# Two attention blocks on one core: regrouping DMAs split over two queues, the local projection moved ahead, and results of the next-to-last image moved

## The chip, the cores and the metric

One Trainium2 chip; the kernel runs on one of its cores. The metric is device time in microseconds, the median over runs of the same program.

## The reference, cut to what matters

The input x is 8 images of 32 x 32 tokens with 256 channels, float32. Two blocks follow each other, each behind a group norm (32 groups of 8 channels over all tokens of an image) and each added to its input.

```
x = x + local(gn(x))     # 32 rows of 32 tokens, 8 heads of 32: softmax(q k^T / sqrt(32)) v per row and head, then w_proj, b_proj
x = x + gamma * wide(gn(x))   # over all N = 1024 tokens of an image:
#   q = x Wq, k = x Wk (256 -> 32), v = x Wv (256 -> 256)
#   energy[i, j] = k_i . q_j;  attn = softmax over j;  out_i = sum_j attn[i, j] v_j
```

## The kernel before, in words

The kernel is written engine by engine, with semaphores placed by hand; each engine runs its own list in order, so the order of work is the order of the code. Products are made of float16 halves: a value is held as a high part and a low part, and a product takes three matmuls (`split3`, L275 to L277). PSUM is used as two tensors of four banks, pa and pb.

The local block is called a, the wide one b. For an image, block a has: load (SP), transposes and group norm ("a"), keys and queries (`a_project_qk`, chunks 0 and 1 of 512 tokens, four column groups d each; d = 0, 1 are queries and are copied by ScalarE, d = 2, 3 are keys and are copied by VectorE), values (`a_project_v`), scores, softmax, results (`a_output`), then the **regrouping**: VectorE ends the low parts of the results (`a_out_low`, L1010), and sixteen DMAs of 64 KB (`a_regroup`, L335, four r by four s) move them from the buffer before_turn to the buffer turned, so that channels lie on partitions. Then comes the **local projection** (`a_projection`, four groups j of 12 matmuls, form pa<-wp_h,turned), and the residual (`a_residual`, L1019, VectorE), which makes x1.

Block b takes x1: transposes and group norm ("b": statistics and aggregation L941 and L947, mean and variance over groups as two small matmuls on TensorE, L436 and L441, the scale on GpSimd, the normalisation on ScalarE, the split on VectorE L974 and L976), keys and queries (`b_project_qk`), the stacks (`b_stacks`, four DMAs), eight energy pairs (`b_energy`, L589), of which VectorE takes the row maxima (`b_maximum`, L1039; pair it + 1 waits for the maximum of pair it, since they share the banks), the maxima as two rows, eight transposed energy pairs (`b_energy_T`, L607), of which ScalarE takes the exponential (L833, L834) and VectorE the low part e_l (`b_exp_low`, L1054), values (`b_project_v`), and eight results (`b_output`, for each tile `it` of 128 rows 8 x 3 matmuls of 257 columns over `jt`), scaled by ScalarE (`b_scaled`, L843, with VectorE's factor, L1059 and L1061) and added by GpSimd (`b_add`, L1251) to y, into which GpSimd has copied x1 (`b_keep`, L1244). The stores of y are issued in pairs j of tiles by SP (j = 0, 1, 2) and ScalarE (j = 3); `b_keep` of pair j waits for the store of the image before.

Images overlap. `all_steps` calls two half-steps for i, `first(i)` and `second(i)`, on every engine. `first(i)` has energies of image i beside results of image i - 1, local results of image i + 1 and the norm of image i + 2; `second(i)` has transposed energies and values of image i, regrouping, local projection, norm b of image i + 1, and keys, queries, values and scores of image i + 2. i = 0, 1 are written out, i = 2, 3, 4 are a hardware loop (`Fori`, L246), i = 5 to 8 are written out again. The flags b, o, m, f of the half-steps say whether the images i, i - 1, i + 1, i + 2 exist. The last image is treated apart: its results 0 to 5 are made jt by jt right behind the exponentials (`outputs_behind`), in banks that are free by then (`result_bank`).

Lines that the steps below touch: `result_bank` L282, `a_regroup` L326, SP's half-steps L367 to L380, `a_projection` L546, `b_output` L611, TensorE's half-steps L632 to L701, ScalarE's L845 to L884, VectorE's L1063 to L1118, GpSimd's L1253 to L1271.

Of the kernel before, what the change touches and what calls it, by code (L numbers as in the profile page):

```python
# [55 lines left out]
def build(nc, x, w_qkv, w_proj, b_proj, wq1, wk1, wv1, gamma, ident_d, group_d, masks_d, out):  # L56
# [3 lines left out]
    with ExitStack() as ctx:  # L60
# [123 lines left out]
        a_ox = sem("a_ox")  # L184

# [95 lines left out]

        def result_bank(b, it):  # L282
# [58 lines left out]
        def _(sp):  # L341
# [53 lines left out]
            a_regroup(sp, 0, (0, 1))  # L395
# [11 lines left out]
        def _(pe):  # L407
# [203 lines left out]
            def b_output(b, it, b_next, jts=range(TILES)):  # L611

                if last_image(b):
                    pe.wait_ge(b_el, nth(b, 8, jts[-1] + 1))

                    if it >= 6:
                        pe.wait_ge(b_part, nth(b, 8, it - 5))
# [14 lines left out]
            def first(i, b, o, m, f):  # L632

                for it in range(4):
                    if o and not last_image(i - 1): b_output(i - 1, it, b, range(0, 4))
                    if b and it == 2: b_energy(i, 1, m)
                    if o and not last_image(i - 1): b_output(i - 1, it, b, range(4, 8))
                    if f and it == 1: transposes("a", i + 2, range(4))
                    if b and it >= 1: b_energy(i, (0, 2, 3)[it - 1], m)
                for it in range(4, 8):  # L640
# [4 lines left out]
                    if o: b_output(i - 1, it, b, range(0, 4))  # L645
# [4 lines left out]
                    if o: b_output(i - 1, it, b, range(4, 8))  # L650
                    if b and it < 7: b_energy(i, it, m)
                    if f and it == 4: group_mean("a", i + 2)

            def outputs_behind(b, jts):

                for jt in jts:
                    if jt == 0:

                        pe.wait_ge(b_vl, nth(b, 4, 4))
                    for it in range(6):  # L660
                        b_output(b, it, False, (jt,))

            def second(i, b, o, m, f):
# [15 lines left out]
                if b and f and not image(i, 0): b_project_v(i, (3,))  # L679
                if last_image(i): outputs_behind(i, (1,))  # L680
                if f: a_project_qk(i + 2, 1, (1,))
                if b: b_energy_T(i, 5)
                if last_image(i): outputs_behind(i, (2,))
                if m: a_projection(i + 1, f, (0, 1))
                if b: b_energy_T(i, 6)
                if last_image(i): outputs_behind(i, (3,))
                if m: a_projection(i + 1, f, (2,))
                if m: transposes("b", i + 1, (0, 1))
                if m: a_projection(i + 1, f, (3,))
                if b: b_energy_T(i, 7)  # L690
                if last_image(i): outputs_behind(i, range(4, 8))
                if f: a_project_qk(i + 2, 1, (2,))
                if f: a_project_qk(i + 2, 1, (3,))
                if m: transposes("b", i + 1, (2, 3))
                for j in range(4):
                    if m and j == 2: group_var("b", i + 1)
                    if f: a_project_v(i + 2, (j,))
                    if m and j == 0: group_mean("b", i + 1)
                if f: a_scores(i + 2)
                for c in range(CHUNKS):  # L700
                    if m: b_project_qk(i + 1, f, c)  # L701
# [54 lines left out]
        def _(act):  # L756
# [44 lines left out]
            def a_out_high(b):  # L801
                act.wait_ge(a_o, nth(b, 1, 1))

                after(act, a_ox, nth(b, 256, 0))
# [53 lines left out]
            def second(i, b, o, m, f):  # L858
# [11 lines left out]
                if b and f and not image(i, 0): b_v_high(i, (3,))  # L870
                if f: a_copy_q(i + 2, 1)
                for jt in range(5, 7):
                    if b: b_exponential(i, jt)
                if m: copy_T("b", i + 1, (0, 1))
                if b: b_exponential(i, 7)
                if m: copy_T("b", i + 1, (2, 3))
# [43 lines left out]
            a_regroup(act, 0, (2, 3))  # L920
# [14 lines left out]
        def _(dve):  # L935
# [49 lines left out]
            def a_maximum(b, c):  # L985
# [4 lines left out]
                if c == 0:  # L990

                    after(dve, a_ox, nth(b, 256, 0))
# [70 lines left out]
            def first(i, b, o, m, f):  # L1063
                if m: a_maximum(i + 1, 1)
                if o: b_factor(i - 1, 0)
                if m: a_row_sum(i + 1, 0)
                if b: b_maximum(i, 0)
                if o: b_factor(i - 1, 1)
                if m: a_row_sum(i + 1, 1)
                if b: b_maximum(i, 1)  # L1070
                if o: b_factor(i - 1, 2)
# [4 lines left out]
                if o: b_factor(i - 1, 3)  # L1076
# [3 lines left out]
                if o: b_factor(i - 1, 4)  # L1080
# [3 lines left out]
                if o: b_factor(i - 1, 5)  # L1084
                if b: b_maximum(i, 6)
                if o: b_factor(i - 1, 6)
# [4 lines left out]
            def second(i, b, o, m, f):  # L1091
# [7 lines left out]
                if b and not f: b_v_low(i, (3,))  # L1099
                if b: b_exp_low(i, 2)  # L1100
                if f: a_copy_k(i + 2, 0)
                if b: b_exp_low(i, 3)
                if b: b_exp_low(i, 4)
                if b and f and not image(i, 0): b_v_low(i, (3,))
                if m: a_residual(i + 1, (0,))
                if b: b_exp_low(i, 5)
                if m: a_residual(i + 1, (1, 2))
                if b: b_exp_low(i, 6)
                if m: a_residual(i + 1, (3,))
                if m: stats("b", i + 1, (0,))  # L1110
                if f: a_copy_k(i + 2, 1)
                if m: stats("b", i + 1, (1,))
# [94 lines left out]
        def _(pool):  # L1207
# [82 lines left out]
            a_probabilities(0, 1)  # L1290
            add_bias(1)
# [37 lines left out]
```

## Time and profile before

| | us |
|---|---|
| median of 3 runs | 676.5 (675.51 to 678.45) |
| the profiled execution, its own time | 673.91 |
| its span, first to last instruction | 672.1 |
| TensorE busy | 590.7 |
| VectorE busy | 470.2 |
| ScalarE busy | 349.4 |
| GpSimd busy | 196.2 |

All rows are from one execution. Times count from the span's start. In a timeline a row is a start, a duration, the engine (PE is TensorE, DVE VectorE, ACT ScalarE, POOL GpSimd, SP SyncE; a q behind the name is the engine's DMA queue), the line, the operation and its tiles; in brackets stands how long the engine sat idle before it and who ended that. Matmuls are pipelined, so a row of 0.27 us is followed by the next 0.11 us later.

### The profile page before, as it was taken

How to read it: one execution, taken by the hardware profiler on the slowest of the kernel's cores; microseconds unless marked ns; L12 is line 12 of the kernel's file. 1: busy time of each engine (PE TensorE's matmuls, PEld its weight loads, DVE VectorE, ACT ScalarE, POOL GpSimd, SP SyncE). 2: the span in 40 equal slices, each digit the busy share in tenths (PEclk: the TensorE clock that was granted, in tenths of full speed). 3: DMA queues.
4: the chain of work that ended last, by engine and by line, in shares of the span. 5: the costliest groups of instructions: out<-in, count | busy, mean ns of one | idle time of the engine just before them, and what ended most of it. 6: DMA issues, size and time to landing. Idle time of an engine off the chain costs nothing.

```text
span 672.1 us, 15153 instructions
## 1 busy us (share of the span) xinstructions
PE 590.7 (88%) x5859; PEld 426.5 (63%) x5859; DVE 470.2 (70%) x765; ACT 349.4 (52%) x486; POOL 196.2 (29%) x194
## 2 busy tenths in 40 slices
PE   2797845799999999999999999999999999649987
PEld 2465723457775777668676777577766767427756
DVE  4565378577868787788868796878768875764462
ACT  2662245375358643874278535865287414641462
POOL 7422034103352324420450335231452142001303
PEclk9799867899999999999999999999999999769989
DMA  6113323033223313224223313331322231201101
GB/s 211 38 41 96 95 63 86 20 76 96 55 81 102 103 25 96 76 60 111 62 67 89 94 46 87 93 91 44 96 68 60 53 84 60 51 1 41 48 0 63
DMA packets 40308, 47.53 MB, mean 71 GB/s; under 512 B 6848, under 2 KB 32320, under 8 KB 40256
## 3 DMA queue, kind: packets, MB, share of 16 engines
q1 hardware_dynamic: 35280, 41.37, 23.5%
q10 hardware_dynamic: 4976, 5.44, 2.6%
q8 instruction: 35, 0.57, 0.4%
q14 instruction: 17, 0.14, 0.1%
HBM read 10.09 MB, written 8.39 MB: 27 GB/s over the span
## 4 chain that ended last, share of the span: by engine, by line
PE 66%; DVE 16%; issue 5%; ACT 4%; SPq 4%; DMA 3%; ACTq 1%; POOL 0%; DVEq 0%; POOLq 0%
PE pb L275 10%; PE pb L276 9%; PE pb L277 9%; PE pa L275 6%; PE pa L277 6%; PE pa L276 6%; DVE max_neg L1039 4%; PE pa L541 4%; PE pb L589 3%; PE pa L508 3%; PE pb L607 3%; SPq L335 3%; PE pb L429 2%; PE pa L429 2%; DVE ast L941 2%
## 5 line engine op out<-in xcount | busy, mean ns | idle before, releaser
L275 PE MATMUL pb<-v_h,e_h 128*128 128x257 f16 x464 | 127.5, 275 | 0.0
L277 PE MATMUL pb<-v_h,e_l 128*128 128x257 f16 x464 | 126.5, 273 | 0.0
L276 PE MATMUL pb<-v_l,e_h 128*128 128x257 f16 x464 | 126.1, 272 | 0.0
L1039 DVE TENSOR_REDUCE max_neg<-pb 128x1 f32<-128x1024 f32 x64 | 77.6, 1213 | 56.2 <-PE pb L589 56.0
L1054 DVE TENSOR_TENSOR e_l<-e,e_h 128x1024 f16<-128x1024 f32 x64 | 77.9, 1224 | 19.4 <-ACT e L834 18.0
L843 ACT ACTIVATE qk_h<-pb,y_fac 128x256 f32<-128x256 f32 x58 | 27.5, 474 | 110.0 <-DVE y_fac L1061 109.6
L1251 POOL TENSOR_TENSOR y<-qk_h,y 128x256 f32<-128x256 f32 x64 | 46.4, 728 | 117.7 <-ACT qk_h L843 117.6
L834 ACT ACTIVATE e<-pb,f_energy 128x1024 f32<-128x1024 f32 x64 | 71.3, 1114 | 16.3 <-PE pb L607 16.3
L1232 POOL TENSOR_TENSOR xb<-xin,bias 128x2048 f32<-128x2048 f32 x8 | 36.3, 4533 | 143.4 <-DVE x L1019 142.8
L1237 POOL TENSOR_TENSOR before_turn<-before_turn,a_rinv 128x1024 f32<-128x1024 f32 x16 | 30.6, 1913 | 107.0 <-DVE a_rinv L1000 101.2
L833 ACT ACTIVATE e_h<-pb,f_energy 128x1024 f16<-128x1024 f32 x40 | 44.5, 1114 | 22.9 <-PE pb L607 22.9
L275 PEld LDWEIGHTS pb<-v_h,e_h 128*128 128x128 f16 x464 | 45.7, 99 | 13.6 <-issue 1.4
L276 PEld LDWEIGHTS pb<-v_l,e_h 128*128 128x128 f16 x464 | 45.7, 98 | 12.0
L589 PE MATMUL pb<-q_stack,k_stack 96*128 96x512 f16 x128 | 39.9, 394 | 15.0 <-DVE max_neg L1039 13.7
L275 PE MATMUL pa<-a_nh,wqkv_h 128*128 128x512 f16 x128 | 49.2, 384 | 1.4 <-POOL a_nl L1225 1.3
L277 PEld LDWEIGHTS pb<-v_h,e_l 128*128 128x128 f16 x464 | 44.6, 96 | 6.9
L277 PE MATMUL pa<-a_nh,wqkv_l 128*128 128x512 f16 x128 | 49.0, 383 | 0.0
L276 PE MATMUL pa<-a_nl,wqkv_h 128*128 128x512 f16 x128 | 49.0, 383 | 0.0
L607 PE MATMUL pb<-k_stack,q_stack 98*128 98x512 f16 x128 | 39.3, 389 | 10.9 <-ACT e L834 9.5
L1225 POOL TENSOR_TENSOR a_nl<-a_xT,a_nh 128x512 f16<-128x512 f32 x32 | 37.4, 1168 | 26.1 <-ACT a_xT L780 26.1
L275 PE MATMUL pb<-wqkv_h,a_nh 128*128 128x256 f16 x128 | 35.6, 278 | 2.6 <-ACT v_tok L795 2.6
L778 ACT ACTIVATE a_nh<-a_xT,anb,ar 128x512 f16<-128x512 f32 x32 | 25.7, 804 | 21.9 <-POOL anb L1214 21.9
(152 smaller groups left out, 1365.8 us busy)
## 6 DMA issues: line engine op xcount, KB each, us to landing
xin<-in_x SPq DMA_DIRECT2D x15, 512.0 KB, 4.6
diag<-qkT SPq DMA_DIRECT2D x60, 128.0 KB, 2.4
diag<-turned SPq DMA_DIRECT2D x60, 128.0 KB, 2.4
turned<-before_turn SPq DMA_DIRECT2D x120, 64.0 KB, 2.0
out<-y SPq DMA_DIRECT2D x24, 256.0 KB, 2.2
out<-y ACTq DMA_DIRECT2D x8, 256.0 KB, 2.1
q_stack<-qk_hl SPq DMA_DIRECT2D x8, 128.0 KB, 2.3
k_stack<-qk_hl SPq DMA_DIRECT2D x8, 128.0 KB, 2.3
```

The costliest lines, as they stand in the source:

```text
L275: nc.tensor.matmul(out_ap, lh, rh, start=start, stop=False)
L276: nc.tensor.matmul(out_ap, lh, rl, start=False, stop=False)
L277: return nc.tensor.matmul(out_ap, ll, rh, start=False, stop=stop)
L589: last = nc.tensor.matmul(pb[:, c, :], k_stack[0:96, it * P:(it + 1) * P], q_stack[0:96, c * CHUNK:(c + 1) * CHUNK], start=True, stop=True)
L607: last = nc.tensor.matmul(pb[:, c, :], q_stack[0:98, jt * P:(jt + 1) * P], k_stack[0:98, c * CHUNK:(c + 1) * CHUNK], start=True, stop=True)
L833: nc.scalar.activation(e_h[:, jt, :], src, ACT.Exp, scale=f_energy[:, 0:1])
L834: nc.scalar.activation(e32[:, jt % 2, :], src, ACT.Exp, scale=f_energy[:, 0:1]).then_inc(b_exp, 1)
L1039: nc.vector.tensor_reduce(max_neg[:, it:it + 1], pb[:, 0:2, :].rearrange("p a n -> p (a n)"), X, ALU.max, negate=True).then_inc(b_max, 1)
L1054: nc.vector.tensor_tensor(e_l[:, jt, :], e32[:, jt % 2, :], e_h[:, jt, :], ALU.subtract).then_inc(b_el, 1)
L1225: nc.gpsimd.tensor_tensor(a_nl[:, ct, cols], a_xT[:, ct, cols], a_nh[:, ct, cols], ALU.subtract).then_inc(n_["a"]["nl"], 1)
L1232: nc.gpsimd.tensor_tensor(xb[:], xin[:], bias[:].unsqueeze(1).broadcast_to([P, TILES, CH]), ALU.add).then_inc(a_xb, 1)
L1251: nc.gpsimd.tensor_tensor(y[:, it, :], y_part[:, it % 2, :], y[:, it, :], ALU.add).then_inc(b_y, 1)
```

## The change

The sixteen regrouping DMAs are no longer all issued by SP: `a_regroup` takes the semaphore to tell, SP issues r = 0, 1 on `a_ox` and GpSimd r = 2, 3 on the new `a_oxp`, in `second` right behind `b_keep(i, 3)`; in the prologue GpSimd takes them in ScalarE's place. Who waited for `a_ox` now waits for both. In the half-steps with a next-next image (i = 0 to 5) TensorE follows the new list `second_with_next`: the local projection's first two groups stand behind keys-and-queries chunk 1 d = 0, ahead of the fifth transposed energy pair, and d = 1, 2, 3 come behind; norm b's transposes, and on ScalarE and VectorE the copies, residuals and statistics, move ahead with it. In `first` VectorE takes the second maximum ahead of the local row sum, and TensorE the mean of norm a one step later. For image 6 (`next_to_last`) results 0 to 3 are made jt by jt in `second(6)`, in pa, and results 4 to 7 in halves in `first(7)`. Results 6 and 7 of image 7 use two banks of pb. The half-steps cut below are SP's `second`, TensorE's `first` and `second`, VectorE's `first` and GpSimd's `second`, in this order.

```diff
         def result_bank(b, it):
             if last_image(b):
-                it = it % 6
-                return pa[:, it, :] if it < 4 else pb[:, it - 2, :]
+                return pa[:, it, :] if it < 4 else pb[:, (it - 2) % 4, :]
+            if next_to_last(b) and it < 4:
+                return pa[:, it, :]
             return pb[:, 2 + it % 2, :]
...
-        def a_regroup(eng, b, rs):
+        def a_regroup(eng, b, rs, landed):
...
-                    eng.dma_start(o_dst[32 * s:32 * s + 32, r], o_src[32 * r:32 * r + 32, :, s]).then_inc(a_ox, 16)
+                    eng.dma_start(o_dst[32 * s:32 * s + 32, r], o_src[32 * r:32 * r + 32, :, s]).then_inc(landed, 16)
...
             def second(i, b, o, m, f):
-                if m: a_regroup(sp, i + 1, range(4))
+                if m: a_regroup(sp, i + 1, (0, 1), a_ox)
...
             def a_projection(b, b_next, js):
                 for j in js:
-                    pe.wait_ge(a_ox, nth(b, 256, 256))
+                    pe.wait_ge(a_ox, nth(b, 128, 128))
+                    pe.wait_ge(a_oxp, nth(b, 128, 128))
...
             def b_output(b, it, b_next, jts=range(TILES)):
...
+                elif next_to_last(b) and it < 4:
+                    pe.wait_ge(b_el, nth(b, 8, jts[-1] + 1))
+                elif next_to_last(b):
+                    if it >= 6:
+                        pe.wait_ge(b_part, nth(b, 8, it - 1))
...
             def first(i, b, o, m, f):
                 for it in range(4):
-                    if o and not last_image(i - 1): b_output(i - 1, it, b, range(0, 4))
+                    if o and b and not next_to_last(i - 1): b_output(i - 1, it, b, range(0, 4))
+                    if next_to_last(i - 1): b_output(i - 1, 4 + it // 2, b, range(it % 2 * 4, it % 2 * 4 + 4))
...
+            def second_with_next(i, b):
+                a_project_qk(i + 2, 1, (0,))
+                a_projection(i + 1, True, (0, 1))
+                b_energy_T(i, 4)
+                if not image(i, 0): b_project_v(i, (3,))
+                b_energy_T(i, 5)
+                a_projection(i + 1, True, (2,))
+                transposes("b", i + 1, (0, 1))
+                a_projection(i + 1, True, (3,))
+                b_energy_T(i, 6)
+                a_project_qk(i + 2, 1, (1,))
+                transposes("b", i + 1, (2, 3))
+                a_project_qk(i + 2, 1, (2,))
+                b_energy_T(i, 7)
+                a_project_qk(i + 2, 1, (3,))
+                a_project_v(i + 2, (0,))
+                group_mean("b", i + 1)
...
                 if b: b_energy_T(i, 3)
-                if f: a_project_qk(i + 2, 1, (0,))
+                if f:
+                    second_with_next(i, b)
+                    return
                 if last_image(i): outputs_behind(i, (0,))
+                if next_to_last(i): outputs_behind(i, (0,), (0, 1))
...
                 for j in range(4):
+                    if next_to_last(i) and j == 0: outputs_behind(i, (4, 5, 6), (0, 1))
                     if m and j == 2: group_var("b", i + 1)
                     if m and j == 0: group_mean("b", i + 1)
+                    if next_to_last(i) and j == 0:
+                        outputs_behind(i, (7,), (0, 1))
+                        outputs_behind(i, (0, 1), (2, 3))
+                    if next_to_last(i) and j == 2: outputs_behind(i, range(2, 8), (2, 3))
...
             def first(i, b, o, m, f):
+                early = o and next_to_last(i - 1)
                 if o: b_factor(i - 1, 0)
+                if early:
+                    for it in (1, 2, 3):
+                        b_factor(i - 1, it)
                 if m: a_row_sum(i + 1, 0)
                 if b: b_maximum(i, 0)
-                if o: b_factor(i - 1, 1)
+                if o and not early: b_factor(i - 1, 1)
+                if b: b_maximum(i, 1)
                 if m: a_row_sum(i + 1, 1)
-                if b: b_maximum(i, 1)
...
             def second(i, b, o, m, f):
                 if b: b_keep(i, 3)
+                if m: a_regroup(pool, i + 1, (2, 3), a_oxp)
                 if f: add_bias(i + 2)
                 if m: rstd("b", i + 1)
```

Three places show the order. TensorE, `second(1)`, behind the fourth transposed energy pair, before (a row is a place in the list, the line, the operation, its tiles, and the semaphores it waits for):

```order
853 L276 MATMUL pa<-a_nl,wqkv_h 128x512
854 L277 MATMUL pa<-a_nh,wqkv_l 128x512
855 L607 MATMUL pb<-k_stack,q_stack 128x512 [waits b_exp]
856 L607 MATMUL pb<-k_stack,q_stack 128x512
857 L275 MATMUL pb<-wv_h,b_nh 128x256 [waits b_vl]
```

and in the change:

```order
853 L277 MATMUL pa<-a_nl,wqkv_h 128x512
854 L278 MATMUL pa<-a_nh,wqkv_l 128x512
855 L276 MATMUL pa<-wp_h,turned 128x256 [waits a_ke,a_oxp,a_ox]
856 L277 MATMUL pa<-wp_l,turned 128x256
857 L278 MATMUL pa<-wp_h,turned 128x256
```

The projection (tiles wp_h, wp_l, turned) took the place of the energy pair and of the values behind it, and waits for both semaphores of the regrouping.

GpSimd in the loop, around the end of the copies of x1 into y (L1244 before, L1296 in the change), before:

```order
89 L1240 REGISTER_ALU
90 L1244 COPY y<-x 128x512
91 L1229 ISA
92 L1232 TENSOR_TENSOR xb<-xin,bias 128x2048
93 L1212 TENSOR_TENSOR br<-bve,minus_half 128x2
```

and in the change:

```order
93 L1296 COPY y<-x 128x512
94 L236 REGISTER_ALU
95 L340 DMA turned<-before_turn 32x2x512 x8
96 L1281 ISA
97 L1284 TENSOR_TENSOR xb<-xin,bias 128x2048
98 L1264 TENSOR_TENSOR br<-bve,minus_half 128x2
```

Eight DMAs stand between the last copy and the bias sum.

TensorE in `second(6)`, around the mean of norm b of image 7, before:

```order
2301 L429 MATMUL pb<-ident,x 128x128 [waits bn_xt,a_x1]
2302 L429 MATMUL pb<-ident,x 128x128 x3
2303 L436 MATMUL pb<-bmv,group_avg 128x2 [waits bn_mv]
2304 L441 MATMUL pb<-be,group_avg 128x2 [waits bn_var]
2305 L275 MATMUL pb<-b_nh,wqk_h 128x512 [waits b_exp,bn_nl]
```

and in the change:

```order
2343 L277 MATMUL pa<-v_l,e_h 128x257
2344 L278 MATMUL pa<-v_h,e_l 128x257
2345 L441 MATMUL pb<-bmv,group_avg 128x2 [waits bn_mv]
2346 L276 MATMUL pa<-v_h,e_h 128x257 [waits b_el]
2347 L277 MATMUL pa<-v_l,e_h 128x257
```

Results of image 6 now stand on both sides of the mean; the variance is place 2364.

## Rows read from the trace of the kernel before

**Rows 1.** The page: busy time of each engine; granted TensorE clock in 40 slices.

```profile
PE 590.7 (88%) x5859; PEld 426.5 (63%) x5859; DVE 470.2 (70%) x765; ACT 349.4 (52%) x486; POOL 196.2 (29%) x194
...
PEclk9799867899999999999999999999999999769989
```

**Rows 2.** One image: us; busy PE, PEld, DVE, ACT, POOL (count); granted clock; DMA; GB/s.

```profile
394.00:467.00 73.00, 70.88 (x734) 52.05 (x732) 57.63 (x93) 42.88 (x61) 23.47 (x24) 1.00 0.29 77
```

**Rows 3.** Timeline of TensorE: its gaps in one image, and one ahead.

```profile
325.13 0.60 PE L589 MATMUL pb<-q_stack,k_stack 96*128 96x512 f16 x2 [0.93 <-DVE max_neg L1039]
...
332.51 0.38 PE L436 MATMUL pa<-amv,group_avg 128*128 128x2 f32 x2 [0.49 <-DVE amv L947]
...
375.76 0.38 PE L436 MATMUL pb<-bmv,group_avg 128*128 128x2 f32 x2 [0.64 <-DVE bmv L947]
...
143.45 0.28 PE L275 MATMUL pa<-wp_h,turned 128*128 128x256 f16 x1 [1.52 <-DMA turned<-before_turn]
```

**Rows 4.** Timeline of VectorE: the local row sum between two maxima.

```profile
322.39 1.21 DVE L998 TENSOR_REDUCE a_rsum<-before_turn 128x32 f32<-128x1024 f32 x1
```

**Rows 5.** SP's queue: the regrouping in one image, and all issues of its line.

```profile
350.81 10.29 SPq L335 DMA_DIRECT2D turned<-before_turn  x16
...
L335 SPq DMA_DIRECT2D turned<-before_turn x120: 585/597/1069, 67.3 to 578.1; - x120
...
DMA to landing us min/median/max: 2.0/2.0/3.4
```

**Rows 6.** Timeline of TensorE and GpSimd around the local projection, same image.

```profile
357.99 0.38 PE L275 MATMUL pa<-a_nh,wqkv_h 128*128 128x512 f16 x1
...
358.64 0.38 PE L275 MATMUL pa<-a_nh,wqkv_h 128*128 128x512 f16 x1
...
362.99 0.27 PE L275 MATMUL pa<-wp_h,turned 128*128 128x256 f16 x1
...
352.87 1.38 POOL L1244 COPY y<-x 128x512 f32<-128x512 f32 x1 [2.34 <-issue]
370.87 4.54 POOL L1232 TENSOR_TENSOR xb<-xin,bias 128x2048 f32<-128x2048 f32 x1 [16.62 <-DVE x L1019]
```

**Rows 7.** Timeline of GpSimd in the prologue.

```profile
82.57 4.51 POOL L1232 TENSOR_TENSOR xb<-xin,bias 128x2048 f32<-128x2048 f32 x1 [27.80 <-DVE x L1019]
```

**Rows 8.** Timeline of GpSimd, TensorE and VectorE: image 6's second half-step.

```profile
570.77 1.02 POOL L1244 COPY y<-x 128x512 f32<-128x512 f32 x1 [2.96 <-issue]
...
580.10 0.39 PE L275 MATMUL pa<-wp_h,turned 128*128 128x256 f16 x1 [0.54 <-DMA turned<-before_turn]
...
593.59 0.38 PE L436 MATMUL pb<-bmv,group_avg 128*128 128x2 f32 x2 [2.80 <-DVE bmv L947]
594.81 0.59 PE L441 MATMUL pb<-be,group_avg 128*128 128x2 f32 x2 [0.84 <-DVE be L959]
600.17 0.61 PE L275 MATMUL pb<-b_nh,wqk_h 128*128 128x512 f16 x1 [4.77 <-DVE b_nl L976]
...
594.67 1.22 DVE L1054 TENSOR_TENSOR e_l<-e,e_h 128x1024 f16<-128x1024 f32 x1
```

**Rows 9.** Busy time and granted clock behind gaps, columns as in rows 2.

```profile
142.00:144.00 2.00, 0.55 (x5) 0.51 (x6) 1.44 (x2) 2.00 (x3) 0.00 (x0) 1.00 0.61 140
...
582.00:584.00 2.00, 2.00 (x11) 1.40 (x10) 1.01 (x2) 0.00 (x0) 0.00 (x0) 0.50 0.00 0
600.00:604.00 4.00, 3.83 (x10) 1.35 (x11) 2.52 (x6) 0.60 (x1) 0.00 (x0) 0.50 0.01 4
642.00:646.00 4.00, 3.92 (x20) 2.68 (x20) 3.22 (x4) 1.11 (x1) 0.00 (x0) 0.57 0.00 0
```

**Rows 10.** Timeline of TensorE and VectorE: energies and maxima of image 7.

```profile
610.49 0.60 PE L589 MATMUL pb<-q_stack,k_stack 96*128 96x512 f16 x2
612.51 0.59 PE L589 MATMUL pb<-q_stack,k_stack 96*128 96x512 f16 x2
...
629.49 1.23 DVE L1039 TENSOR_REDUCE max_neg<-pb 128x1 f32<-128x1024 f32 x1 [0.51 <-PE pb L589]
```

More of the change, by code:

```diff
@@ L184, in build @@
         a_ox = sem("a_ox")
+        a_oxp = sem("a_oxp")
         b_copy = sem("b_copy")
@@ L634, in first @@
                 for it in range(4):
-                    if o and not last_image(i - 1): b_output(i - 1, it, b, range(0, 4))
+                    if o and b and not next_to_last(i - 1): b_output(i - 1, it, b, range(0, 4))
+                    if next_to_last(i - 1): b_output(i - 1, 4 + it // 2, b, range(it % 2 * 4, it % 2 * 4 + 4))
                     if b and it == 2: b_energy(i, 1, m)
-                    if o and not last_image(i - 1): b_output(i - 1, it, b, range(4, 8))
+                    if o and b and not next_to_last(i - 1): b_output(i - 1, it, b, range(4, 8))
                     if f and it == 1: transposes("a", i + 2, range(4))
@@ L644, in first @@
                         continue
-                    if o: b_output(i - 1, it, b, range(0, 4))
+                    if next_to_last(i - 1): b_output(i - 1, 4 + it // 2, b, range(it % 2 * 4, it % 2 * 4 + 4))
+                    elif o: b_output(i - 1, it, b, range(0, 4))
+                    if f and it == 5: group_mean("a", i + 2)
                     if m and it == 5: a_output(i + 1, f, 0)
@@ L649, in first, with outputs_behind @@
                     if b and it == 7: b_energy(i, it, m)
-                    if o: b_output(i - 1, it, b, range(4, 8))
+                    if o and not next_to_last(i - 1): b_output(i - 1, it, b, range(4, 8))
                     if b and it < 7: b_energy(i, it, m)
-                    if f and it == 4: group_mean("a", i + 2)
-            def outputs_behind(b, jts):
+            def outputs_behind(b, jts, its=range(6)):
                 for jt in jts:
@@ L659, in outputs_behind @@
                         pe.wait_ge(b_vl, nth(b, 4, 4))
-                    for it in range(6):
+                        pe.wait_ge(a_ol, nth(IMAGES, 2, 0))
+                    for it in its:
                         b_output(b, it, False, (jt,))
+            def second_with_next(i, b):
[15 more added lines that the diff above has]
+                group_mean("b", i + 1)
+                a_project_v(i + 2, (1,))
+                group_var("b", i + 1)
+                a_project_v(i + 2, (2, 3))
+                a_scores(i + 2)
+                for c in range(CHUNKS):
+                    b_project_qk(i + 1, True, c)
             def second(i, b, o, m, f):
@@ L802, in a_out_high @@
                 act.wait_ge(a_o, nth(b, 1, 1))
-                after(act, a_ox, nth(b, 256, 0))
+                after(act, a_ox, nth(b, 128, 0))
+                after(act, a_oxp, nth(b, 128, 0))
                 for g in range(2):
@@ L870, in second @@
                 if b and f and not image(i, 0): b_v_high(i, (3,))
+                if b: b_exponential(i, 5)
+                if m and f: copy_T("b", i + 1, (0, 1))
+                if b: b_exponential(i, 6)
+                if m: copy_T("b", i + 1, (2, 3) if f else (0, 1))
                 if f: a_copy_q(i + 2, 1)
-                for jt in range(5, 7):
-                    if b: b_exponential(i, jt)
-                if m: copy_T("b", i + 1, (0, 1))
                 if b: b_exponential(i, 7)
-                if m: copy_T("b", i + 1, (2, 3))
+                if m and not f: copy_T("b", i + 1, (2, 3))
                 if f: a_copy_v(i + 2, (0, 1, 2))
@@ L1075, in first @@
                 if b: b_maximum(i, 3)
-                if o: b_factor(i - 1, 3)
+                if o: b_factor(i - 1, 5 if early else 3)
                 if f: stats("a", i + 2, (1,))
@@ L1079, in first @@
                 if f: group_mean("a", i + 2)
-                if o: b_factor(i - 1, 4)
+                if o and not early: b_factor(i - 1, 4)
                 if b: b_maximum(i, 4)
@@ L1083, in first @@
                 if b: b_maximum(i, 5)
-                if o: b_factor(i - 1, 5)
+                if o: b_factor(i - 1, 6 if early else 5)
                 if b: b_maximum(i, 6)
-                if o: b_factor(i - 1, 6)
+                if o and not early: b_factor(i - 1, 6)
                 if b: b_maximum(i, 7)
```

44 lines of the change are left out of this document (23 added, 21 removed).

## The prediction

> **What bounds the kernel now.** I read the page's busy shares and slices first, then stretches of the main part, then the idle times of TensorE one by one, and last what the other engines and queues did around each. TensorE is busy for 590.7 of 672.1 us, no other engine for more than 470.2 [rows 1]. In the repeated part it is nearly full: one image takes 73.0 us, and TensorE works in 70.9 of them at the full clock (granted 1.00, the 2.4 GHz level) [rows 2]. There a microsecond is won only by closing one of its few gaps, and any new wait of TensorE is paid whole. The clock row of the page also shows where the work thins out: at the start, and from slice 34 on, where image 7 has no next image beside it [rows 1].
>
> The gaps of one image in the repeated part are three [rows 3]: 0.93 us before an energy pair (L589) that waits for the maximum of the pair before, 0.49 us before the group mean of norm a and 0.64 us before that of norm b (both L436). Over images they recur: six of the first kind (0.93 to 1.00), five of the second (0.39 to 0.50), six of the third (0.64 or 0.65), 5.7 + 2.3 + 3.9 = **11.8 us**. The fourth row is a single case: in the first half-step, before the loop, the local projection waits 1.52 us for the regrouped data.
>
> **The change, part by part.** The first gap: VectorE does the local row sum (1.21 us) before the second maximum, and the third energy pair waits for that maximum [rows 4]. The change puts the maximum first. The row sum comes 1.2 us later; it feeds GpSimd, whose result VectorE takes only after two more maxima, so the delay is covered. The mean of norm a moves behind a half result of twelve matmuls; the mean of norm b keeps its neighbours, but its statistics start earlier, since the projection, the transposes and the copies ahead of it do. I count all three gaps as closed: **-11.8**.
>
> What pays for it is the projection's new place. It waits for the regrouping: SP, right behind VectorE's low parts, issues sixteen DMAs in 10.29 us from 350.81, 0.643 us apiece (0.60 busy, at most 1.07), and a DMA lands 2.0 us after its issue (at most 3.4) [rows 5]. TensorE starts the projection at 362.99, just as the last one lands [rows 6]. In the change it stands right behind the group of keys and queries that begins at 357.99; its second half begins at 358.64, so it ends at 359.28 [rows 6]. TensorE is there 3.7 us sooner.
>
> SP's half is ready: eight issues from 350.81 end at 355.95, landed at 358. GpSimd's half cannot start at 350.8. On its queue it stands behind the last copy of x into y, which waits 2.34 us for the store of the image before and ends at 354.25 [rows 6]. No DMA was ever issued from this queue here, so its price has to be bounded. Below: under (359.28 - 354.25 - 2.0) / 8 = 0.38 us apiece nothing waits. Above: 1.07, the longest issue of such a piece on SP. I take SP's 0.643, the nearest row, since piece and pattern are the same, and count the landing from the end of the issue: 354.25 + 8 x 0.643 + 2.0 = 361.4. TensorE would wait 2.1 us, in each of the five half-steps of images 1 to 5: **+10.5**. What is queued behind the DMAs on GpSimd, the bias sum, ran only at 370.87 [rows 6], so it is not late; the two engines that newly wait on both semaphores (ScalarE and VectorE, before they overwrite the source) come one image later and wait for nothing.
>
> The Trainium skill (DMA: Bandwidth & Descriptors, "SWDGE vs HWDGE vs iDMA" and "Latency and other measured facts") says that GpSimd's DMAs have their descriptors written by software and start after about 1 us, SP's after about 0.6. The 0.60 agrees with this trace's SP rows; no run here shows the 1 us. With 1 us apiece the sum, by that page an estimate, would give a wait of 5.0 us in each of those half-steps, 2 us more at the end, and 685 instead of my time.
>
> In the half-step of image 0 GpSimd has no store to wait for; its half lands with SP's near 137, and TensorE comes at 139.3 (the group before ends there by the same spacing). The single gap of 1.52 closes: **-1.5**. Ahead of it, in the prologue, ScalarE loses eight issues and GpSimd, idle there for 27.8 us, gains them [rows 7]. They start with the same source, so at SP's price nothing changes, and at 1.07 they end 8 x 0.43 = 3.4 us later, once.
>
> **The end.** In image 6's second half-step there is no next image. TensorE waits there for exponentials, for the regrouping (0.54), for statistics (2.80 and 0.84) and for the norm (4.77) [rows 8]. The change puts half of image 6's results, 4 x 8 x 3 matmuls at 0.11 = 10.6 us, into these gaps. Step by step: GpSimd is free at 571.79, its half lands at 578.9, and TensorE, behind the sixth energy pair and a piece of results, comes at 579.6, so the projection starts 0.5 sooner. Its first 24 matmuls take 2.6 us at the full clock, 0.11 apiece, but 0.50 was granted (the 1.2 GHz level) while most of them ran, after stretches in which TensorE was mostly idle [rows 8, 9]; with the result pieces between, I expect the full clock and 2 us back. Transposes and statistics follow 1.5 sooner. But then two groups of results stand between the mean and the variance, and the first waits for the last e_l (1.22 on VectorE, queued behind the mean): the variance comes at 596.5 instead of 594.81, and the norm, which waited for that same e_l before, 1.1 us later. The following projection began at 600.17 behind the longest gap, with 0.50 granted [rows 8, 9], and ran 4.9 us; its twelve matmuls of 512 columns take 2.6 at the spacing of rows 6, which I expect with 4 us of results ahead of it. Together this half-step ends **1.3 sooner**.
>
> In image 7's first half-step the energies were spaced by the results: the first at 610.49, the maximum of the eighth at 629.49, 0.64 behind its energy, so 18.4 us for seven steps [rows 10]. With four results left, in halves of 1.33 us, each energy waits for the maximum before it, as between 610.49 and 612.51, where only a half result was in between [rows 10]: 7 x 2.02 = 14.1. **4.2 sooner.** The factors of the four early results come ahead of the first maximum, while VectorE waits for the stacks anyway. The last two results of image 7 change banks and lose a wait that TensorE never showed: nothing.
>
> The sum: -11.8 + 10.5 - 1.5 - 1.3 - 4.2 = **-8.3**. The profiled execution took 673.9, so 665.6; the median of the runs is 2.6 above it, so **668**.
>
> **Rivals.** *GpSimd's queue is slow, the kernel is slower.* In each of five half-steps TensorE then stands at the projection until the second half lands. At 1.07 apiece that is 354.25 + 8.56 + 2.0 = 364.8, a wait of 5.5, five times 27.6; at the end the half lands 2.7 behind TensorE. -11.8 - 1.5 + 27.6 - 5.5 + 2.7 = +11.5: 688. Such a wait may also cost the clock: behind gaps of image 7's own half-step TensorE got 0.57 for four microseconds, 1.7 lost, while around the 1.52 gap it kept 1.00 [rows 9]; five times that gives 697. It decides from a wait of 3.8 us, a price of 0.85. For it: the copy that holds the queue until 354.25, and that a queue with another generator has no reason to match SP. Against it: SP's own 0.60 for the same piece. The page above speaks for it; another of the skill (SBUF — State Buffer, "SBUF: two separate sides") says that VectorE copies in two-port mode shut GpSimd out from writing descriptors, which no row here shows and which would only add.
>
> *GpSimd's queue is quick, below 0.38.* Nothing waits: -11.8 - 1.5 - 5.5 = -18.8: 658. For it: the DMAs may be handed over faster than SP does it; against it: no row.
>
> *The gaps are only put off.* The statistics, maxima and copies leave the places named but meet another wait, and the 11.8 stays: 680, with part of it won 674 to 680. For it: one closed gap lets the next one show; against it: the other engines are busy under 58 of 73 us [rows 2].
>
> **How the numbers follow.** The forecast (a wait of 1 to 3.5 us) has 0.42, and 661 to 675 as its own range; the slow queue 0.33, 679 to 697; the quick one 0.15, 655 to 661; gaps put off 0.10. From 656 to 692 little is left out below, and above it the slow case with the full price of the clock, some 0.12. 0.5% (3.4 us) is about what a measurement can tell from no change: faster has the quick case and most of the forecast, 0.50; the same 0.17; slower 0.33.
>
> **What would show it.** The Pool queue's rows: eight DMAs of the regrouping, their spacing, and when the last lands after 354. At the first projection matmul (its form pa<-wp_h,turned): a wait on a DMA of about 2 us in five half-steps; none would mean the quick case, over 3.8 the slow one. The three gaps of rows 3 gone, 71 us of TensorE work plus that wait between images. At the end, energies of image 7 some 2.0 us apart, a granted clock near 1.00 during its projection, and the variance later behind the mean than 1.2 us. Wrong would be: the 0.93 gap still there, or a new wait elsewhere of the same size.

## The result, and the profile after

| | before | changed |
|---|---|---|
| median, us | 676.0 (674.73 to 678.45, 4 runs) | 696.4 (691.16 to 698.83, 4 runs) |
| profiled execution, span | 672.1 | 694.5 |

The changed kernel is slower by a factor of 1.0287 (95% interval 1.0221 to 1.0353). The forecast was 668; 696.4 lies outside its range of 656 to 692 too, and near the price of the slow-queue rival, whose mechanism is not what happened.

First, from the page after: the busy row of TensorE, VectorE and GpSimd (line 1), the granted clock, and GpSimd's DMA queue (packets, MB, share).

```profile
PE 597.9 (86%) x5859; PEld 429.4 (62%) x5859; DVE 482.7 (70%) x765; ACT 348.3 (50%) x486; POOL 231.2 (33%) x258
...
PEclk9999977699999999999999999999999999999999
...
q0 software_dynamic: 2048, 4.20, 2.3%
```

Beside [rows 1]: VectorE is busy 12.5 us longer with the same 765 instructions, so some became longer. The clock did what I expected at the end (no thin slices), so the loss is not there. Next one image, between the same points of two images, columns as in [rows 2]:

```profile
367.11:442.34 75.23, 71.26 (x734) 52.17 (x732) 59.70 (x93) 42.73 (x61) 27.86 (x31) 1.00 0.28 75
```

75.2 us instead of 73.0, at the full clock: TensorE waits 4.0 us in it, against 2.1 in rows 2. What it waited for, from image 0's first transposed energy to image 6's first energy: first the changed kernel, then the kernel before (us in total, times, longest).

```profile
PE pb L276 <- ACT e L879: 7.0, 6, 1.2
PE pa L513 <- DMA diag<-qkT: 6.8, 6, 1.8
PE pb L595 <- DVE max_neg L1085: 3.8, 5, 0.8
PE pa L276 <- DMA turned<-before_turn: 2.1, 3, 0.7
PE pa L513 <- issue: 1.8, 1, 1.8
PE pb L434 <- DVE v_l L1080: 1.6, 5, 0.3
...
PE pa L276 <- issue: 1.1, 2, 0.6
```

```profile
PE pb L589 <- DVE max_neg L1039: 4.7, 5, 0.9
PE pb L436 <- DVE bmv L947: 3.9, 6, 0.6
PE pa L436 <- DVE amv L947: 2.3, 5, 0.5
PE pa L275 <- DMA turned<-before_turn: 1.5, 1, 1.5
```

Both waits for group means are gone and the one for a maximum is smaller. But two waits that did not exist are larger than all that went: 7.0 us ahead of the values of block a (`a_project_v`, for an exponential) and 6.8 ahead of the scores (L513, for the spread keys). The projection's wait, on which I had put 10.5, is 2.1 + 1.1 = 3.2 (a DMA or, in two images, "issue"). The same places in one image, from the changed kernel's timelines of TensorE, VectorE, GpSimd and SP:

```profile
374.91 0.28 PE L276 MATMUL pa<-wp_h,turned 128*128 128x256 f16 x1 [0.74 <-DMA turned<-before_turn]
...
382.02 0.63 PE L434 MATMUL pb<-ident,x 128*128 128x128 f32 x4 [0.33 <-DVE v_l L1080]
...
390.75 0.28 PE L276 MATMUL pb<-wqkv_h,a_nh 128*128 128x256 f16 x1 [1.16 <-ACT e L879]
...
397.89 3.70 PE L513 MATMUL pa<-diag,qkT 128*32 128x128 f32 x128 [0.83 <-DMA diag<-qkT]
...
384.00 0.75 DVE L1065 SCALAR_TENSOR_TENSOR x<-pa,f_proj,xb 128x512 f32<-128x512 f32 x1 [0.33 <-PE pa L278]
...
386.59 3.95 DVE L1100 TENSOR_TENSOR e_l<-e,e_h 128x1024 f16<-128x1024 f32 x1 [0.65 <-ACT e L879]
...
368.91 4.41 POOL L340 DMA_DIRECT2D turned<-before_turn  x8
384.93 4.53 POOL L1284 TENSOR_TENSOR xb<-xin,bias 128x2048 f32<-128x2048 f32 x1 [11.61 <-DVE x L1065]
...
365.53 5.15 SPq L340 DMA_DIRECT2D turned<-before_turn  x8
```

**Here is the longer VectorE work**: an e_l that takes 1.22 us in its other rows of this image takes 3.95 here, and GpSimd's bias sum (`add_bias`, xb) runs from 384.93 to 389.46 beside it. The e_l ends at 390.54, 1.08 behind the sum's end: about its own length, so it had not moved before. Six e_l of the run take 3.95 to 4.05, one in each half-step of images 0 to 5, each beside a bias sum. Before, the last residual (x) came behind the seventh e_l, and the sum that it releases ran at 370.87 [rows 6] beside statistics and copies out of PSUM. VectorE's timeline of the kernel before, same image:

```profile
368.39 1.23 DVE L1054 TENSOR_TENSOR e_l<-e,e_h 128x1024 f16<-128x1024 f32 x1
369.94 0.75 DVE L1019 SCALAR_TENSOR_TENSOR x<-pa,f_proj,xb 128x512 f32<-128x512 f32 x1 [0.32 <-PE pa L277]
```

The change moved the residuals ahead of that e_l (the last now starts at 384.00), and the sum came with them.

### The profile page after: what moved, and what is told of

Read it like the earlier page. It is cut to its first block, busy times and chain, and to the rows that moved or that the text cites. A ratio compares the mean times of both kernels' runs of the same rounds, so it can differ in the third digit from the quotient of the medians.

```text
span 694.5 us, 15182 instructions
## 1 busy us (share of the span) xinstructions
PE 597.9 (86%) x5859; PEld 429.4 (62%) x5859; DVE 482.7 (70%) x765; ACT 348.3 (50%) x486; POOL 231.2 (33%) x258
## 4 chain that ended last, share of the span: by engine, by line
PE 54%; DVE 18%; issue 7%; ACT 7%; DMA 7%; SPq 3%; POOL 2%; ACTq 0%; DVEq 0%; POOLq 0%
PE pb L276 8%; PE pb L277 7%; PE pb L278 7%; PE pa L546 5%; PE pb L595 4%; PE pa L276 4%; PE pa L277 4%; PE pa L278 4%; DVE max_neg L1085 4%; DVE e_l L1100 4%; PE pa L513 3%; ACT e L879 3%; PE pb L613 3%; DMA diag<-qkT 2%; PE pa L434 2%
## 5 line engine op out<-in xcount | busy, mean ns | idle before, releaser
L276 PE MATMUL pb<-v_h,e_h 128*128 128x257 f16 x448 | 123.5, 276 | 0.0
L278 PE MATMUL pb<-v_h,e_l 128*128 128x257 f16 x448 | 122.5, 273 | 0.0
L277 PE MATMUL pb<-v_l,e_h 128*128 128x257 f16 x448 | 122.2, 273 | 0.0
L1100 DVE TENSOR_TENSOR e_l<-e,e_h 128x1024 f16<-128x1024 f32 x64 | 94.8, 1482 | 20.9 <-ACT e L879 20.1
L595 PE MATMUL pb<-q_stack,k_stack 96*128 96x512 f16 x128 | 41.6, 409 | 17.9 <-DVE max_neg L1085 13.9
L276 PEld LDWEIGHTS pb<-v_h,e_h 128*128 128x128 f16 x448 | 43.9, 98 | 14.0 <-issue 1.7
L277 PEld LDWEIGHTS pb<-v_l,e_h 128*128 128x128 f16 x448 | 44.2, 99 | 12.3 <-issue 0.3
L340 POOL DMA_DIRECT2D turned<-before_turn x64 | 35.5, 562 | 29.5 <-DVE before_turn L1056 29.5
```

What stands on the lines that cost most here:

```text
L276: nc.tensor.matmul(out_ap, lh, rh, start=start, stop=False)
L277: nc.tensor.matmul(out_ap, lh, rl, start=False, stop=False)
L278: return nc.tensor.matmul(out_ap, ll, rh, start=False, stop=stop)
L595: last = nc.tensor.matmul(pb[:, c, :], k_stack[0:96, it * P:(it + 1) * P], q_stack[0:96, c * CHUNK:(c + 1) * CHUNK], start=True, stop=True)
L1100: nc.vector.tensor_tensor(e_l[:, jt, :], e32[:, jt % 2, :], e_h[:, jt, :], ALU.subtract).then_inc(b_el, 1)
```

## Where the 22.4 us of the span went

First energies and first transposed energies of each image (TensorE's timeline) cut the run into pieces; the table has each piece's time less that of the kernel before, for the changed kernel and three of the experiments below (profiled executions, one of each kernel, us, rounded). The column "forecast" has the terms of the prediction's sum, put on the same pieces.

| piece | forecast | changed | e1 | e6 | e4 |
|---|---|---|---|---|---|
| up to image 0's first transposed energy | 0 | 5.8 | 1.1 | 5.6 | 0.7 |
| second half-steps of images 0 to 5 | 5.1 | 19.4 | 8.9 | 1.0 | -1.4 |
| first half-steps of images 1 to 6 | -8.0 | -3.8 | -3.2 | -3.1 | -2.8 |
| second half-step of image 6 | -1.3 | 2.0 | 1.9 | 1.0 | 2.0 |
| first half-step of image 7 | -4.2 | -3.4 | -3.3 | -4.8 | -3.4 |
| from there to the end | 0 | 2.5 | 2.5 | 1.3 | 2.5 |

The widest miss, 14.3 us, lies in the second half-steps.

## The experiments

Theory A after the traces: the bias sum holds the seventh e_l, and behind it the keys' copy, their spreading and the scores are late. Rival B: the new order alone makes the waits. In all, nine kernels ran, each timed beside the kernel before on its chip (ratios are against that, with 95% intervals).

**e1_bias_later: the collision taken away.** The bias sum is needed only an image later.

```diff
             def second(i, b, o, m, f):
                 if b: b_keep(i, 3)
                 if m: a_regroup(pool, i + 1, (2, 3), a_oxp)
+                if b and f: pool.wait_ge(b_el, nth(i, 8, 7))
                 if f: add_bias(i + 2)
```

> The changed kernel, and on GpSimd the bias sum of the next image waits until VectorE has done its seventh e_l. Theory A (the bias sum, released earlier by the moved residuals, holds VectorE's seventh e_l for 2.7 us in six half-steps, and the keys' copy, their spreading and the scores are late behind it): all 64 e_l take 1.22 us again, the scores' wait of 0.8 to 1.8 us goes, 1.2 us on average in six half-steps, about 689 us instead of 696. Theory B (the collision is harmless, the new order alone makes the waits): e_l at 1.22 us, but 694 to 698 us, and the scores wait as before.

684.3 us, 1.0137 (1.0059 to 1.0215): 12 us less than the changed kernel by the medians, 10 by the two ratios, and less than the 689 expected. All e_l on VectorE (busy, mean ns), before the sum was held back and after:

```profile
L1100 DVE TENSOR_TENSOR e_l<-e,e_h 128x1024 f16<-128x1024 f32 x64 | 94.8, 1482 | 20.9 <-ACT e L879 20.1
```

```profile
L1100 DVE TENSOR_TENSOR e_l<-e,e_h 128x1024 f16<-128x1024 f32 x64 | 78.2, 1222 | 20.9 <-ACT e L879 20.1
```

In its trace the wait of the scores for spread keys is gone from all six half-steps. The other two stay as they were, 7.0 and 1.6 us:

```profile
PE pb L276 <- ACT e L879: 7.0, 6, 1.2
...
PE pb L434 <- DVE v_l L1080: 1.6, 5, 0.3
```

So A and B are both true, of different waits. By the table the collision cost 19.4 - 8.9 = 10.5 us; the rest of the 14.5 by which the span is shorter is in the main the piece up to image 0. The scores' wait is 6.8 of the 10.5. In the image shown the second half-step takes 46.79 us in the changed kernel and 45.26 in e1: 0.83 of the difference is the scores' wait, and 0.62 comes ahead of it, around the group mean and variance of norm b, whose statistics stand behind that e_l too.

**e9_bias_in_quarters: how long is VectorE held?**

```diff
-                nc.gpsimd.tensor_tensor(xb[:], xin[:], bias[:].unsqueeze(1).broadcast_to([P, TILES, CH]), ALU.add).then_inc(a_xb, 1)
+                for j in range(4):
+                    ts = slice(2 * j, 2 * j + 2)
+                    last = nc.gpsimd.tensor_tensor(xb[:, ts, :], xin[:, ts, :], bias[:].unsqueeze(1).broadcast_to([P, 2, CH]), ALU.add)
+                last.then_inc(a_xb, 1)
```

> The changed kernel with the bias sum of an image written as four instructions of 512 columns in place of one of 2048, about 1.15 us each, started at the same moment. If the two engines exclude each other per instruction, VectorE's seventh e_l gets in behind the quarter that is running: 1.2 to 2.5 us instead of 3.95 in six half-steps, the scores wait less, 688 to 692 us. If VectorE is held as long as GpSimd has work: 3.95 us or more again, 695 to 698.

685.7 us, 1.0163 (1.0101 to 1.0225), under the 688 to 692 expected and not to be told from e1. The six e_l take 1.93 to 2.03, as expected for the first case. In one image, VectorE's e_l and GpSimd's four quarters, and under them the quarters' durations (min, median, max, ns):

```profile
374.75 1.93 DVE L1100 TENSOR_TENSOR e_l<-e,e_h 128x1024 f16<-128x1024 f32 x1 [0.64 <-ACT e L879]
...
373.10 5.94 POOL L1286 TENSOR_TENSOR xb<-xin,bias 128x512 f32<-128x512 f32 x4 [11.61 <-DVE x L1065]
...
L1286 POOL TENSOR_TENSOR xb<-xin,bias x4: 1258/1266/2250, 373.1 to 377.8; 128x512 f32<-128x512 f32 x4
```

VectorE waits for the quarter that is running, 0.7 us, and then one quarter waits for VectorE (2.25 instead of 1.26): the two exclude each other one instruction at a time. The Trainium skill (SBUF — State Buffer, "Who interferes with whom") says this: a VectorE instruction with two inputs in SBUF and a GpSimd instruction that reads SBUF share one port, and the one that starts first has it to its end. The trace agrees in both orders.

**e6_reordered: the order's own waits.** With e1's wait kept, the transposed energies move, with ScalarE and VectorE in step.

```diff
                 a_project_qk(i + 2, 1, (0,))
+                b_energy_T(i, 4)
                 a_projection(i + 1, True, (0, 1))
-                b_energy_T(i, 4)
+                b_energy_T(i, 5)
                 if not image(i, 0): b_project_v(i, (3,))
-                b_energy_T(i, 5)
                 a_projection(i + 1, True, (2,))
+                b_energy_T(i, 6)
                 transposes("b", i + 1, (0, 1))
                 a_projection(i + 1, True, (3,))
-                b_energy_T(i, 6)
+                b_energy_T(i, 7)
                 a_project_qk(i + 2, 1, (1,))
                 transposes("b", i + 1, (2, 3))
-                a_project_qk(i + 2, 1, (2,))
-                b_energy_T(i, 7)
-                a_project_qk(i + 2, 1, (3,))
+                a_project_qk(i + 2, 1, (2, 3))
```

> The first run's kernel (bias sum held back) with the transposed energies moved: the fifth ahead of the projection, the sixth ahead of the last values, the seventh ahead of the transposes and the eighth ahead of the last three groups of keys and queries, ScalarE and VectorE in step. Theory (the 1.16 us before the values, the 0.32 before a transpose and part of the 0.73 at the projection come only from too little work between an energy and what waits for its exponential): these waits fall to 0.5 us together, 1.7 less in six half-steps, about 674 us instead of 684. Rival (other engines cannot be earlier, the wait moves to the scores or the norm): 681 to 686.

673.4 us, 0.9963 (0.9928 to 0.9999), 11 less than e1. The wait for the exponential is gone, and so is the projection's for the DMA, since an energy pair now fills it. The transposes' wait did not fall but grew, from 1.6 to 3.1 in all (0.67 in one image):

```profile
PE pb L595 <- DVE max_neg L1083: 3.8, 5, 0.8
PE pb L434 <- DVE v_l L1078: 3.1, 5, 0.7
```

Why the exponential was late: the changed order left one group of keys (1.3 us) between the eighth energy pair and the values that need its bank, and ScalarE needs two passes of 1.2 us for that pair. Before, two groups and two transposes stood there. The pair on TensorE and the two passes on ScalarE, from the changed kernel's timelines (the values begin at 390.75):

```profile
387.69 0.60 PE L613 MATMUL pb<-k_stack,q_stack 98*128 98x512 f16 x2
...
388.53 1.16 ACT L878 ACTIVATE e_h<-pb,f_energy 128x1024 f16<-128x1024 f32 x1
389.53 1.17 ACT L879 ACTIVATE e<-pb,f_energy 128x1024 f32<-128x1024 f32 x1
```

**e4_old_second_half and e3_pool_queue_alone: one part at a time.** e4 is the changed kernel with the repeated second half-step in the old order; e3 is the kernel before with the halved regrouping alone. The core of each:

```diff
-                if f:
-                    second_with_next(i, b)
-                    return
+                if f: a_project_qk(i + 2, 1, (0,))
...
                 if b: b_energy_T(i, 4)
+                if b and f and not image(i, 0): b_project_v(i, (3,))
...
```

```diff
-                if m: a_regroup(sp, i + 1, range(4))
+                if m: a_regroup(sp, i + 1, (0, 1), a_ox)
...
+                if m: a_regroup(pool, i + 1, (2, 3), a_oxp)
                 if f: add_bias(i + 2)
```

> The changed kernel with the repeated second half-step back in the old order on TensorE, ScalarE and VectorE; the halved regrouping, the new first half-step and the new end stay. Theory (the order of the second half-step costs 3 us in each of six images, by whatever mechanism): 676 + 3.4 for GpSimd's queue - 5.3 for the first half-steps (0.9 each, as measured) - 1.4 for the end = about 673 us, and no e_l over 1.3 us. Rival (the loss lies in the queue or the first half-step): 685 or more.

> The kernel before with only the regrouping halved between SP and GpSimd, in the prologue too. Theory: no half-step waits more, the wait of 1.5 us in image 0's half-step goes, the prologue waits 2.2 us more and the end takes 2.6 more: about 679 us, e_l at 1.22 us everywhere. Rival (GpSimd's DMAs disturb VectorE and the queues in every half-step): 684 or more, with longer VectorE instructions beside the DMAs.

e4 took 670.8 us, 0.991 (0.9875 to 0.9945): the loss lies in the order of the second half-step, as the table says too. e3 took 674.5, 1.0014 (0.9971 to 1.0057), less than I expected: the halved regrouping alone costs nothing that its runs can show. Neither has an e_l over 1.3.

**e2_no_pool_queue: the new order without GpSimd's queue.** The changed kernel, all sixteen DMAs on SP, in the prologue half on ScalarE.

```diff
                 if m: a_regroup(sp, i + 1, (0, 1), a_ox)
+                if m: a_regroup(sp, i + 1, (2, 3), a_oxp)
...
-                if m: a_regroup(pool, i + 1, (2, 3), a_oxp)
```

> The changed kernel with the regrouping back on SP (16 DMAs) in the half-steps and on SP and ScalarE in the prologue, everything else as changed. If GpSimd's queue only costs at the ends (1.6 us of waiting and its consequences in the prologue, 5 us more in its last instruction) and pays in the half-steps, the ends give back 4.9 us, and the projection waits 3.7 us instead of 0.7 in five half-steps, +15: about 706 us. Theory A adds that the later projection moves the bias sum away from the seventh e_l, which would give up to 7 of them back: 699. If GpSimd's queue is itself what makes the kernel slow: 676 to 685.

717.7 us, 1.0658 (1.0593 to 1.0723), worse than either theory. The projection's place needs the halved regrouping: without it TensorE waits there 9.9 + 8.3 us in all.

```profile
PE pa L276 <- DMA turned<-before_turn: 9.9, 3, 3.4
PE pa L276 <- issue: 8.3, 3, 2.9
```

The collision stays (six e_l of 3.94 to 4.05) with no DMA on GpSimd's queue, so the queue is not its cause: the sum follows the residuals wherever they go.

**e5, e7, e8: towards a faster kernel.** e5 is e4 with the regrouping back on SP (ScalarE in the prologue); e7 is e5 with the first half-step in the old order, so the new end alone; e8 is e5 with VectorE's third maximum ahead of the transpose and the mean of norm b in the middle of the second pair of values. e5 has e2's edit on e4's kernel; e7 and e8 against e5:

```diff
-                if b: b_maximum(i, 1)
                 if m: a_row_sum(i + 1, 1)
+                if b: b_maximum(i, 1)
...
-                    if f and it == 5: group_mean("a", i + 2)
...
+                    if f and it == 4: group_mean("a", i + 2)
```

```diff
-                if m: a_transpose(i + 1, 0)
                 if b: b_maximum(i, 2)
+                if m: a_transpose(i + 1, 0)
...
-                    if f: a_project_v(i + 2, (j,))
-                    if m and j == 0: group_mean("b", i + 1)
+                    if f: a_project_v(i + 2, (j,), (lambda: group_mean("b", i + 1)) if j == 1 else None)
+                    if m and not f and j == 0: group_mean("b", i + 1)
```

> The old order of the second half-step with the new first half-steps and the new end (the fourth run's kernel), and the regrouping back on SP alone, in the prologue on SP and ScalarE. Theory: GpSimd's last instruction takes 0.8 us again instead of 6.1, so the end is 2.6 to 2.9 us shorter; image 0's half-step waits for the regrouping again, about 1.5 us; no other half-step waits for it: 1 us less than the fourth run's kernel, about 670, if that was 671. Rival: GpSimd's half also saved time inside the half-steps, then 674 or more.

> The kernel before with the new end alone: results of image 6 in the gaps of its second half-step, four left for image 7's first; both half-steps in the old order, the row sum ahead of the second maximum, no DMA on GpSimd's queue. Theory from the trace of the changed kernel (energies of image 7 take 3.4 us less, the half-step ahead of them 1.6 more): 1.5 to 2 us less than before, 674. Rival (my forecast's 5.5): 670.

> The fifth run's kernel (old second half-step, new first half-step, new end, no DMA on GpSimd's queue) with its last two gaps of an image addressed: VectorE takes the third maximum ahead of the transpose of the first probabilities, and TensorE forms the mean of norm b in the middle of the second pair of values instead of ahead of it. Theory: 0.77 and 0.64 us go in six images, 8 us, about 661 us. Rival (the transpose is then late for the local output, or the variance late for the norm, and the wait moves): 665 to 670.

| | us | against before |
|---|---|---|
| e5 | 668.5 | 0.9882 (0.9845 to 0.9920) |
| e7 | 673.8 | 0.9976 (0.9940 to 1.0012) |
| e8 | 666.9 | 0.9904 (0.9867 to 0.9940) |

e5, with only the new first half-step and the new end, takes 1.2% less than the kernel before, and its whole interval lies under 1; the end alone is no measurable gain (e7). e8 missed its 661 and came inside its rival's 665 to 670: the two waits closed, and TensorE idles 0.49 us in its steady image instead of 1.47, but its busy time rose from 70.74 to 71.23, so the image only fell from 72.2 to 71.7, and against before it is no better than e5.

What GpSimd's queue costs at the end: the last store is issued on ScalarE's queue, and from its start to the end of the span it is 2.6 us before, 5.5 in the changed kernel, 2.6 in e5. Of each the span and that row:

```profile
core 0 of [0], span 672.1 us
...
669.54 0.38 ACTq L302 DMA_DIRECT2D out<-y  x1
```

```profile
core 0 of [0], span 694.5 us
...
689.04 0.38 ACTq L307 DMA_DIRECT2D out<-y  x1
```

```profile
core 0 of [0], span 666.7 us
...
664.16 0.38 ACTq L307 DMA_DIRECT2D out<-y  x1
```

All six kernels with DMAs on GpSimd's queue show 5.5, all five without 2.6.

## Why the prediction was wrong, point by point

**"What is queued behind the DMAs on GpSimd, the bias sum, ran only at 370.87 [rows 6], so it is not late."** This step failed, and it cost the most. I asked whether the sum would be late, not whether it would be early and beside what. It cost 10.5 us (e1, by the table). The trace of before could have warned me. There a VectorE product of one column, two inputs in SBUF, takes as little as 0.16 us, but 1.06 beside a GpSimd subtraction (339.46 to 340.63), and ends just behind it (VectorE's and GpSimd's timelines of the kernel before):

```profile
339.59 1.06 DVE L1061 TENSOR_TENSOR y_fac<-y_inv,f_out 128x1 f32<-128x1 f32 x1
...
339.46 1.17 POOL L1225 TENSOR_TENSOR a_nl<-a_xT,a_nh 128x512 f16<-128x512 f32 x1 [1.77 <-ACT a_xT L780]
```

I cited the page of the Trainium skill that has the rule (SBUF — State Buffer), but for VectorE against GpSimd's descriptors only.

**The second half-step had no term for what the move uncovers.** This is the second step that failed: without the collision, e1 is still slower than the kernel before. I priced the work that moved and its wait, not what it had covered: the eighth exponential (1.16 us, six times) and a transpose (0.32, five times). e6 shows that the first came from the order, since another order of the same work closes it; the transposes' wait it did not close. My rival "the gaps are only put off" had this mechanism, at a tenth of the chance, and stopped at "the 11.8 stays"; new waits of 1.16 + 0.32 + 0.74 an image are more than the 2.1 that went.

**"I count all three gaps as closed: -11.8."** The two for group means closed (e4, which has the old second half-step, has only that of norm b). The one for a maximum moved: the third energy pair no longer waits 0.93, but the fourth waits 0.77 for the third maximum, which stands behind a transpose on VectorE (341.41, 1.25 us; the maximum follows at 342.58). e8 closed it by taking the maximum first. The first half-steps gave 3.8 us in all, where my terms for them came to 8.0. The single wait of 1.52 in image 0's half-step did close.

**The stall at the projection: +10.5** was too large; it was 0.57 to 0.74 five times, 3.2. GpSimd issues its eight DMAs in 4.41 us, 0.55 apiece, where I took SP's 0.643; and I counted the landing (2.1 measured) from the end of the last issue instead of its start. The Trainium skill's 1 us (DMA: Bandwidth & Descriptors, "Latency and other measured facts") is the time to such a DMA's first byte; as a price apiece, which I made of it, no row bears it out. Nor do SP's rows bear out its 0.6, as I said: their 0.60 [rows 5] is how long an issue takes, not the time to a first byte. e2 shows that the split itself was needed.

**The prologue** waits 1.63 us at the projection, inside my 0 to 3.4. Another 3.7 us up to image 0's transposed energies are the clock: the same 136 matmuls keep TensorE busy for 7.38 us before and 11.10 in the changed kernel. First before, then changed, columns as in [rows 2] (the first stretch also holds the 1.73 us of waiting behind the last matmul, the second ends at its last matmul):

```profile
116.96:127.48 10.52, 7.38 (x136) 4.62 (x136) 5.30 (x7) 1.94 (x2) 2.47 (x5) 0.86 0.01 2
```

```profile
119.00:131.53 12.53, 11.10 (x136) 6.44 (x136) 3.67 (x3) 0.91 (x1) 2.49 (x5) 0.50 0.01 2
```

The granted clock stays at 0.50, the 1.2 GHz level, behind the same energies with waits of 1.41 between them. e3 and e6 show this too (6.0 and 5.6 us later there), e1, e4 and e9 with the same prologue do not (1.1, 0.7, -1.3). So this part is not shown to be the change's; what decides it stays open.

**The end.** Half right. The projection began 0.4 us later in its half-step, not 0.5 sooner, but the mean came 12.2 us behind it instead of 13.5, and the projection ran at the full clock, as forecast. Then the variance came 6.0 behind the mean, not the 4.4 of my working: results ahead of it wait 1.97 for the last e_l. And image 7's first energy waits 2.8 for the stacks, which two whole results covered before. Of the changed kernel's TensorE:

```profile
614.10 0.38 PE L441 MATMUL pb<-bmv,group_avg 128*128 128x2 f32 x2 [0.82 <-DVE bmv L992]
616.45 0.28 PE L276 MATMUL pa<-v_h,e_h 128*128 128x257 f16 x1 [1.97 <-DVE e_l L1100]
...
620.11 0.28 PE L446 MATMUL pb<-be,group_avg 128*128 128x2 f32 x2
...
624.82 0.39 PE L276 MATMUL pb<-b_nh,wqk_h 128*128 128x512 f16 x1 [0.45 <-DVE b_nl L1021]
...
633.85 1.03 PE L595 MATMUL pb<-q_stack,k_stack 96*128 96x512 f16 x2 [2.78 <-DMA k_stack<-qk_hl]
```

So 2.0 lost where I had 1.3 gained; image 7's energies gave 3.4 of the 4.2; and the 2.9 us more that the program's end takes with DMAs on GpSimd's queue had no term.

## What to carry to other kernels

When a step is moved, list everything that its end releases, on every engine, and look at what will then run beside it; "not late" is no answer for work that can come too early. A gap that closes shows the next one, so price the work between each producer and its consumer in the new order, with the duration of the pass that must fit in between. Look for one operation with two durations in the trace of before: the long one can point to a shared resource before a change runs into it.

## What was not expected of the hardware

- VectorE's subtraction with two SBUF inputs stood still until the running GpSimd instruction had ended: 3.95 us instead of 1.22, and 1.93 against quarters. Statistics (0.68 us) and copies out of PSUM (0.64 to 0.69) beside the same sum kept their durations (before and e1).
- A DMA on GpSimd's queue was cheaper to issue than on SP (0.54 against 0.60 us, medians of one image) and landed as fast (2.1 us). But its use makes the program's end 2.9 us longer, once.
- In the changed kernel the scores of image 3, the last ahead of the hardware loop, stop for 1.8 us six matmuls before their end, marked "issue" (e6 shows 1.7 at the same place, e1 0.6 there and 1.0 in the image after). No run here tells why.
